# An attention and expert kernel on one core: the order of the first loads, dummies and small operations is changed

## The reference, cut to what matters

```python
xn = _layernorm(x, axis=-1)                     # x: 16 sequences x 256 tokens x 128
q, k, v = _lora(xn, W, A, B)                    # x @ W.T + x @ B.T @ A.T * 2, three times
s = einsum(q, k) / sqrt(8) + alibi + causal mask     # 16 heads of 8 elements
attn = softmax(s) @ v, then @ Wp.T
logits = xn @ Wr + br                           # routing, 8 experts
g = silu(relu(xi @ W1[i] + b1[i]) @ W2[i] + b2[i])   # the expert of the largest logit; b-terms of all
out = x + attn * g
```

## Time and profile before

| | |
|---|---|
| median of 3 runs | 313.18 us (312.63 to 316.03) |
| the profiled execution | 310.46 us |
| its span, first to last instruction | 308.6 us |
| mean granted TensorE clock | 0.987 |
| TensorE (matmul) busy | 94% of the span |
| VectorE, ScalarE, GpSimd busy | 69%, 67%, 46% |

### The profile page before, as it was taken

How to read it: one execution, slowest core, us unless ns; L and a number is a source line. 1 busy time by engine, 2 the same in 40 slices (tenths; PEclk the granted TensorE clock), 3 DMA queues, 4 the chain that set the end, 5 groups by cost and what they waited for, 6 DMA issues and landing times.

```text
span 308.6 us, 13101 instructions
## 1 busy us (share of the span) xinstructions
PE 289.7 (94%) x5319; PEld 221.6 (72%) x5319; DVE 213.1 (69%) x478; ACT 207.1 (67%) x379; POOL 140.9 (46%) x215
## 2 busy tenths in 40 slices
PE   7999999879897999999999999999999999998983
PEld 3656557748575887888788788878878888875652
DVE  4586897797994665665757566575756656677943
ACT  2343164564668787787778778777877877578961
POOL 3243363115155467646655564665456442325500
PEclk9999999999999999999999999999999999998996
DMA  7589489681224132413323241332324222027531
GB/s 198 152 222 210 121 247 271 211 235 32 71 66 118 49 97 66 117 52 84 92 66 88 57 118 51 91 84 56 98 50 117 57 77 76 12 79 219 152 97 34
DMA packets 46811, 33.89 MB, mean 110 GB/s; under 512 B 5048, under 2 KB 44216, under 8 KB 46624
## 3 DMA queue, kind: packets, MB, share of 16 engines
q1 hardware_dynamic: 42520, 26.80, 32.3%
q0 software_dynamic: 2496, 5.12, 6.1%
q10 hardware_dynamic: 1736, 1.14, 1.6%
HBM read 13.17 MB, written 6.75 MB: 65 GB/s over the span
## 4 chain that ended last, share of the span: by engine, by line
PE 68%; DVE 16%; DMA 5%; issue 4%; ACT 4%; POOL 2%; SPq 1%; ACTq 0%; DVEq 0%; POOLq 0%
PE bank L1355 13%; PE bank L1363 11%; PE bank L1305 10%; PE bank L1253 10%; DVE row_max L814 5%; PE bank L1166 3%; PE bank L1261 3%; PE bank L1339 3%; PE bank L1173 2%; PE bank L1325 2%; ACT probs L753 2%; DVE xn_all L1054 2%; PE bank L1347 2%; PE bank L1182 2%; PE bank L1233 2%
## 5 line engine op out<-in xcount | busy, mean ns | idle before, releaser
L814 DVE TENSOR_REDUCE row_max<-bank 128x2 f32<-128x512 f32 (+3 forms) x176 | 105.8, 635 | 23.5 <-PE bank L1241 19.5
L753 ACT ACTIVATE probs<-bank 128x512 f32<-128x512 f32 (+1 forms) x176 | 90.0, 558 | 34.3 <-PE bank L1261 33.6
L1253 PE MATMUL bank<-qk_stack 64*64 64x64 bf16 (+3 forms) x1024 | 60.7, 236 | 3.3 <-ACT probs L753 1.5
L1233 PE MATMUL bank<-qk_stack 64*64 64x64 bf16 (+3 forms) x1024 | 61.1, 235 | 0.7 <-DMA qk_stack<-parts 0.7
L520 POOL DMA_INDIRECT xs_slot<-normalised_rows,from_row x39 | 38.5, 987 | 41.7 <-PE bank L1261 33.0
L1036 DVE TENSOR_TENSOR hT<-bank,w_slots 128x512 f32<-128x512 f32 x39 | 27.0, 691 | 33.6 <-PE bank L1355 33.6
L534 POOL DMA_INDIRECT expert_rows<-y_slot,token_of x39 | 38.6, 991 | 24.9 <-DVE y_slot L1042 15.0
L1253 PEld LDWEIGHTS bank<-qk_stack 64*64 64x64 bf16 x1024 | 34.1, 107 | 19.6 <-issue 7.7
L729 ACT ACTIVATE w_slots<-w_all 128x1156 f32 x39 | 45.5, 1167 | 3.4 <-issue 1.2
L1305 PE MATMUL bank<-probs,v_diag 128*32 128x64 f32 (+3 forms) x1024 | 46.5, 307 | 1.3 <-issue 1.1
L1355 PE MATMUL bank<-xsT_slot,w_slots 128*128 128x128 f32 x312 | 44.3, 285 | 0.0
(11 more groups left out here) (135 smaller groups left out, 380.8 us busy)
## 6 DMA issues: line engine op xcount, KB each, us to landing
qk_stack<-parts SPq DMA_DIRECT2D x120, 64.0 KB, 2.0
qk_stack<-parts SPq DMA_DIRECT2D x32, 128.0 KB
w_all<-w_experts SPq DMA_DIRECT2D x8, 512.0 KB, 5.9
normalised_rows<-xn_all SPq DMA_DIRECT2D x4, 512.0 KB, 7.6
xn_all<-expert_rows SPq DMA_DIRECT2D x8, 256.0 KB, 5.0
out<-xn_all SPq DMA_DIRECT2D x7, 256.0 KB, 2.3
x_all<-x SPq DMA_DIRECT2D x3, 512.0 KB, 7.8
xs_slot<-normalised_rows,from_row POOLq DMA_INDIRECT x39, 2.9
```

The source lines that it names most:

```text
L753: act.activation(probs[:, m % PROBS, 0:w], bank[:, 0:w], ACT.Exp).then_inc(emptied, 1)
L814: dve.tensor_reduce(row_max[b % 2][:, n, pairs[0]:pairs[-1] + 1], bank[:, 0:ln_u * len(pairs)].rearrange("p (c k) -> p c k", k=ln_u), AX.X ...
L1233: pe.matmul(bank[to, c * ln_u:(c + 1) * ln_u], q[rows, p, n * BLK:(n + 1) * BLK], k[rows, p, 0:(n + 1) * BLK], start=(c == 0), stop=False, ...
L1253: pe.matmul(bank[rows, c * ln_u:(c + 1) * ln_u], k[rows, p, kb * BLK:(kb + 1) * BLK], q[rows, p, kb * BLK:], start=(c == 0), stop=False, s ...
```

## The change

It touches the first 25 us of the lists, and one line of the statistics that is used three times:

- ACT issues w_dense ahead of lora; SP waits for both to land before it issues the chunks of x behind the first.
- The two dummies ahead of the turns are moved to the ten at the beginning (12 in one row).
- The constant rows of the first stack are issued by ACT behind `deviation(0)` and a `normalise`, no longer ahead of them. The load of `br` stands behind the stores of sequence 1's k, ahead of that of `b1`.
- Tile 1 is normalised by ScalarE and tile 2 by VectorE. The chain to `rstd` has one operation less in each group of statistics (two fused operations for three).
- w_v, which only `project_v` needs, is put together behind the scaling of q's weights, and TensorE waits for it there.
- The third part of sequence 0 is made on VectorE, behind three of the eight moments of chunk 2. GpSimd waits for it before it makes that of sequence 1.

```diff
-NORM_VEC, NORM_ACT = (0, 1), (2, 4, 5)
+NORM_VEC, NORM_ACT = (0, 2), (1, 4, 5)
...
             sp.dma_start(cf[:, 0:P], const_f32[:, 0:P]).then_inc(S["ident_in"], 16)
+            sp.wait_ge(S["dense_in"], 32)
             load_x(1, 4, 8)
...
-            third_part(0)
+            pool.wait_ge(S["part3_done"], 1)
             third_part(1)
...
+            act.dma_start(dense[:, :], w_dense).then_inc(S["dense_in"], 16)
             act.dma_start(lora_sb, lora).then_inc(S["dense_in"], 16)
-            act.dma_start(dense[:, :], w_dense).then_inc(S["dense_in"], 16)
...
-                follow(dve.tensor_tensor(ln[:, 6, g], ln[:, 6, g], ln[:, 1, g], ALU.mult), group, 5)
-                follow(dve.tensor_scalar(ln[:, 6, g], ln[:, 6, g], -0.5, 1.5, ALU.mult, ALU.add), group, 6)
-                follow(dve.tensor_tensor(rstd[:, g], ln[:, 5, g], ln[:, 6, g], ALU.mult), group, 7)
+                follow(dve.scalar_tensor_tensor(ln[:, 6, g], ln[:, 6, g], -0.5, ln[:, 1, g], ALU.mult, ALU.mult), group, 5)
+                follow(dve.scalar_tensor_tensor(rstd[:, g], ln[:, 6, g], 1.5, ln[:, 5, g], ALU.add, ALU.mult), group, 7)
...
             moments(1, 4, 8)
             remainder(0)
-            then(moments(2, 8, 16))
+            moments(2, 8, 11)
+            dve.wait_ge(S["part2_done"], 1)
+            dve.tensor_tensor(parts[:, 0, 2], rem[:, 0], parts[:, 0, 1], ALU.subtract).then_inc(S["part3_done"], 1)
+            then(moments(2, 11, 16))
             remainder(1)
```

More of the change, by code:

```diff
@@ L610, in _ @@
         def _(act):
+            act.dma_start(dense[:, :], w_dense).then_inc(S["dense_in"], 16)
             act.dma_start(lora_sb, lora).then_inc(S["dense_in"], 16)
-            act.dma_start(dense[:, :], w_dense).then_inc(S["dense_in"], 16)
             act.wait_ge(S["zero_src"], 1)
             act.activation(ln[:, 7, 0:1], zeros[:, 0:1], ACT.Sqrt)
-            load_const_rows(act, 0, 0, 1)
             def deviation(group):
@@ L667, in counts @@
                 act.activation(tile_counts[:, :, :], bank[:, 0:2].unsqueeze(2).to_broadcast([P, 2, P]), ACT.Copy).then_inc(emptied, 1)
-            act.dma_start(br_sb[:, :], br.partition_broadcast(P)).then_inc(S["br_in"], 16)
             deviation(0)
-            normalise(2)
+            normalise(1)
+            load_const_rows(act, 0, 0, 1)
             keep_xT(0)
@@ L688, in _ @@
             store_k(act, 1, 2)
+            act.dma_start(br_sb[:, :], br.partition_broadcast(P)).then_inc(S["br_in"], 16)
             act.dma_start(b1_sb[:, :, :], b1).then_inc(S["b1_in"], 16)
@@ L867, in _ @@
             dve.wait_ge(S["lora_ps"], 1)
[L868 to L872, removed]
+            for n in range(2):
+                last = dve.scalar_tensor_tensor(w_eff[:, n, :], pv_bank[:, n * P:(n + 1) * P], LORA_SCALE, w_raw[:, n, :], ALU.mult, ALU.add)
             then(last)
             dve.tensor_scalar(w_eff[:, 0, :], w_eff[:, 0, :], float(DH) ** -0.5, None, ALU.mult).then_inc(S["w_eff_done"], 1)
+            dve.scalar_tensor_tensor(w_v[:, :, :], pv_bank[:, 2 * P:3 * P].rearrange("p (a x) -> p a x", a=2), LORA_SCALE,
+                                     w_raw[:, 2, :].rearrange("p (a x) -> p a x", a=2), ALU.mult, ALU.add).then_inc(S["w_eff_done"], 1)
             moments(1, 4, 8)
             remainder(0)
-            then(moments(2, 8, 16))
+            moments(2, 8, 11)
+            dve.wait_ge(S["part2_done"], 1)
+            dve.tensor_tensor(parts[:, 0, 2], rem[:, 0], parts[:, 0, 1], ALU.subtract).then_inc(S["part3_done"], 1)
+            then(moments(2, 11, 16))
             remainder(1)
@@ L1140, in warm @@
                     pe.matmul(bank[:, :], cold[:, 0:P], cold.unsqueeze(1).to_broadcast([P, 2, 2 * D]), start=True, stop=True)
-            warm(10, vec_bank[3])
+            warm(12, vec_bank[3])
             pe.wait_ge(S["dense_in"], 32)
@@ L1388, in spread_rows @@
                 last.then_inc(full, 1)
-            warm(2, vec_bank[3])
             pe.wait_ge(S["ident_in"], 16)
@@ L1396, in _ @@
             project(1)
+            pe.wait_ge(S["w_eff_done"], 2)
             project_v(0)
```

## The result

The changed kernel is slower: median 320.3 us of six executions (316.54 to 324.15) against 314.37 of six of the kernel before (312.63 to 317.62), ratio 1.0183, 95% interval 1.0127 to 1.0239. The forecast was 314.0, with a range up to 316.0. The profiled execution took 320.61 us.

What follows compares the result with a forecast made beforehand. It took TensorE, 94% busy, as the bound, so front gains reach the end: 310.46 - 0.7 - 1.0 - 0.2 + 2.7 = 311.3 profiled, 314.0 as a median (313.18 + 0.8), range 311.2 to 316.0.

Steps and rivals of the forecast that it cites:

- The dummies and the dense weights: Twelve dummies end at 6.35 with the weights landed, LoRA products end at 8.0; alone, turns come 1.1 sooner.
- What x's first chunk pays: Loaded alongside the dense weights, x's first chunk lands 0 to 0.75 later, taken as 0.65.
- the lower bound of 0.3: Gain up to the projection of sequence 0: 0.7 forecast, 0.3 if x is 0.4 later still, 1.1 if not late.
- The clock in front: Without the hole, sequence 0's projections run at 2.4 GHz, 1.06 for 2.06: gain 1.0, bounds 0 and 1.3.
- the first rival: The clock stays low in front, so the gain of 1.0 is missing: 315.0, chance 0.2.
- the prediction's own sign of being wrong: Among the signs that the forecast is wrong: the projections still take 0.46 each.
- From the first part to unit 0: First part of sequence 0 at about 10.5 for 12.19, scores' first matmul at about 16.7 for 18.43.
- the fourth rival: The front does not move, as x's chunks or constant rows come later; stall remains: 315.7, chance 0.05.
- The third part on VectorE and the later chunks of x: Sequence 0's third part moved to VectorE, and x's chunks 1 and 2 starting some 3 us later: both cost 0.
- The load of br: br lands at about 25.5, VectorE wants it at 22.46; projection of sequence 2 starts 2.7 later, bounds 0 and 3.2.
- a rival of 0.08: Third rival: the clock falls in the stall for br, each projection costs 1.0 more, about 2.5 in all: 316.5, chance 0.08.

Runs made afterwards that it cites:

- e15_new_loads_only: The kernel before with only the changed kernel's new order of front loads, br still early; ratio 1.0019 to the kernel before.
- e6_old_loads: The changed kernel with br early and all other front loads in their order of before; 331.41, ratio 0.9957 to the kernel before.
- e2_br_late: The kernel before with br alone moved behind the stores of k of sequence 1; 318.69, ratio 1.0233 to the kernel before.
- e7_before_held: The kernel before with 11 dummies at two places in the first round where the clock had fallen; 331.26, ratio 0.9849 to the kernel before.
- e4_bridge: The changed kernel with br early and nine dummies ahead of the turns, over the 2.03 us of idle; 320.46, ratio 1.0236 to the kernel before.
- e16_br_late_held: The kernel before with br loaded behind the stores of k and 18 dummies ahead of unit 6; ratio 1.0114 to the kernel before.
- e10_stall_held: The changed kernel, br late, with 9 dummies ahead of the turns, 26 for 15 ahead of the first unit, 18 ahead of unit 6; 315.7, ratio 1.0104.
- e12_fill_again: The changed kernel with br early, 9 dummies ahead of the turns, 26 for 15 ahead of the first unit, third chip; 315.4, ratio 0.9953.
- e3_hold: The changed kernel with 18 dummies ahead of unit 6 of sequence 0, br still late; 317.09, ratio 1.0108 to the kernel before.
- e1_br_early: The changed kernel with br loaded by ACT ahead of the first deviation, as before the change; 314.8, ratio 1.0124 to the kernel before.
- e11_after_again: The changed kernel itself, measured again on the third chip; median 320.95, 1.024 of the median before.
- e5_fill: The changed kernel with br early, nine dummies ahead of the turns, 26 for 15 ahead of the first unit; 329.28, ratio 0.9888.

## Why the prediction was wrong, by its steps

**The dummies and the dense weights: right, and better than forecast.** The LoRA products ended at 6.39 for 8.0; weights and lora had landed before 5.46.

**What x's first chunk pays: too small.** I took 0.65 out of a range that ended at 0.75; it paid 1.12. In `e15_new_loads_only` it landed at 4.79 and in `e6_old_loads`, with the weights behind lora again, at 3.74. With this the turns started at 8.42, the constant rows' two issues ended at 9.20 for 8.74, and the projection started 0.34 sooner than before, at the lower bound of 0.3.

**The clock in front: failed.** The level did rise in the row of dummies. That the missing hole did it is not what the other profiles say. It rose with ten dummies and a hole too: they took 3.68 in `e2_br_late` (a hole of 2.25 behind them), and in `e7_before_held`, behind a hole of 1.53, the LoRA products took 0.93 for 1.65. And in `e15_new_loads_only` it stayed low without a hole (ten dummies in 4.45, the LoRA products directly behind them in 1.65). Executions differ here, and the prediction had read one. The step failed on what stood behind: the prediction had TensorE busy until 8.0 and turning at once; with the products done at 6.39 and x later, 2.03 us of idle came in between, and the level fell in it. Quicker LoRA products made the hole longer. The gain of 1.0 was 0: the first rival came true, and with 0.47 for each projection the prediction's own sign of being wrong.

**From the first part to unit 0: not carried through.** The prediction passed every gain at the first part on to unit 0 (10.5 to 16.7). The interval is no constant: 6.2 us before, 6.6 in the changed kernel, 7.0 in `e4_bridge`, 6.4 in `e6_old_loads`. The last pair of SP's issues of stores started at 15.53 in the changed kernel, at 15.43 before, though the first part was 0.34 sooner. So unit 0 did not move, as in the fourth rival.

**The third part on VectorE and the later chunks of x: no price seen,** as forecast. VectorE made the third part at 13.94 and began the remainder of sequence 1 at 15.64 (15.81 before). No run tests either by itself.

**The load of br: the place was right, the term half of the loss.** VectorE and TensorE waited where it was said. It landed 6.7 us from issue (4.9 in `e2_br_late`, 5.9 to 7.1 in the other four) where I took 5.0 after b1's 5.4. At equal clock the late br costs 3.35 +- 0.7 (`e2_br_late`), 3.0 +- 0.5 (`e16_br_late_held`), 3.6 +- 0.5 (`e10_stall_held` over `e12_fill_again`) and 4.1 +- 0.8 (`e3_hold` over `e1_br_early`), the last three with dummies in the stall, against 2.7 forecast and a bound of 3.2. So the term was too small, and it held nothing for the clock. The Trainium skill (DMA: Bandwidth & Descriptors, "Anatomy of one DMA") has about 2.0 as the fixed cost of a transfer, in a fit for the path of GpSimd's transfers, while br went by ScalarE's queue; no run comes near it in this place.

**The step that decided it: the clock in the stall, left to a rival of 0.08.** The clock fell in the stall, and the sum had nothing for it. The prediction named the place, the price of a projection (2.07 for 1.06 came) and the point from which it decides, a stall of over about 2 us, while its own term made the stall 2.7. By its own numbers that was the likeliest case and not a mishap. In the first 75 us of the profiles, every idle time of TensorE of over 2 us at the high level had a fall in it or at most 2.2 us behind it; of the shorter ones some had and some had not. `e3_hold` and `e16_br_late_held` are the test: with TensorE busy through the stall, 1.011 and 1.011; without, 1.018 and 1.023 (1.017 and 1.009 against 1.019 and 1.022 between the medians of all executions, so that `e3_hold` alone would not carry it). `e10_stall_held` against `e11_after_again`, 5.2 us on one chip, says the same.

By the prediction's own prices the fourth rival (no gain in front, 315.7) and the third's 2.5 make 318.2; measured are 320.3. The rival was also only in the stall. Five executions of the changed kernel have clocks from 0.952 to 0.969, that is 24.1 us at the low level on the mean, against 15.2 in eleven executions of before on another chip; 8.9 x 0.30 = 2.7. With some 3.0 for the wait this makes 5.7; measured are 5.9 between the medians. That it fits so well is partly luck: 6.8 us of the 32.9 that the profiled execution of the changed kernel was at the low level lie at 8.0 to 14.9, where the kernel before was mostly as slow without the record showing it.

**What stays open.** Why the level falls more often behind the new front, if it does: the runs with br early and the new front stand at 1.0124 and 1.0062, and only falls were seen to differ (at equal clock 0.5 +- 0.7 and 0.0 +- 0.5 us over before, across different fronts). And the two best versions (`e5_fill`, 0.9888 and 0.9953 on two chips, and `e7_before_held`, 0.9849 on the slower chip) are not shown to be faster: between the medians of all executions they are 0.990, 1.006 and 0.996.

## What to carry to other kernels

Before a small load is moved back, look for the engine that reads it and count the landing at the traffic of that place, not at that of its old one; the reader's whole queue stands behind it. Price an idle time of TensorE twice, once as a wait and once as what the next microseconds cost at 1.2 GHz (here 0.3 us or a little more for each; 3 to 10 us in most falls, 24 in one), and look for the hole that opens when one is closed. And when loads and a hand-written list are shifted against each other, look in the first rounds for idle time that no semaphore explains.

## What the runs showed of the hardware

- The clock fell in idle times of 1.5 to 4.3 us (at 8.0, 25.1 and 62.6 in the changed kernel), but also where TensorE was never idle:

```profile
31.00:33.00 2.00, 2.00 (x27) 0.67 0.51 129
32.00:42.00 10.00, 10.00 (x83) 0.67 0.55 141
```

These are windows of `e1_br_early`: it fell at 31.7 in a row of short matmuls, the same that the kernel before ran through at the high level. The Trainium skill (TensorE: Matmul & The Clock Gate, "Part 1: The HAM clock gate") ties the level to how busy TensorE is; the falls in idle times agree, this one shows that the busy share of the profile is not the whole measure.
- The same kernel varies by it: the kernel before ranges from 309.13 at a mean clock of 0.990 to 317.27 at 0.960 on one chip.
- The record of the granted clock reads 1.00 until its first event: before the change the projections took 3.68 us for eight with 1.00 in every window of the front, and now 3.75 with 0.50 beside them. In front the durations tell the level.
- TensorE stood for 1.1 to 3.0 us without a semaphore where q1 filled the DMA engines or had just done so (105 to 114% in the 1.75 us ahead of it and 23% during it in the kernel before), and in one profile the place had moved with the loads. The Trainium skill (Runtime: NRT & Kernel Launch, "Instruction fetch mechanics") has each engine fetch its instructions by DMA in blocks and calls the cost of a further block mostly hidden; if these idle times are such fetches, which is not shown, they are not hidden here.
